# Last expert layer: rows stored by token and gathered by expert, slot owners from one-hot matmuls; router logits inside the norm, last group of residual norms by VectorE

## What is computed

```python
def _ln(x, g, b, eps=1e-05):
    mu = mean(x); v = mean((x - mu) ** 2)
    return (x - mu) * rsqrt(v + eps) * g + b

def _moe(x, wg, w1, b1, w2, b2):              # E = 8, FF = 1024
    S = L * N; cap = S // E                    # 2048 tokens, 256 rows per expert
    gates = softmax(xf @ wg); idx = argmax(gates)
    mask1 = one_hot(idx, E)
    loc = sum((cumsum(mask1, 0) - 1.0) * mask1, -1)    # place among the tokens of its expert
    keep = loc < cap
    slot = where(keep, idx * cap + loc, E * cap)
    disp = zeros((E * cap, D)).at[slot].set(xf, mode='drop')
    h = einsum('ecd,edf->ecf', disp, w1) + b1
    y = einsum('ecf,efd->ecd', h, w2) + b2
    return where(keep, gate_val * y[slot], 0.0)

y1 = _ln(x + _mha(x), ln1_g, ln1_b)
y2 = _ln(y1 + _moe(y1), ln2_g, ln2_b)          # and then x = x + y2
```

## Time and profile before

| | us |
|---|---|
| median of 3 runs | 2350.74 (2348.56 to 2352.39) |
| the profiled execution | 2351.17, its span 2349.3 |
| norm ahead of the last expert layer (`npa`) | 2124.5 to 2148.9 |
| its logits, routing and slots | 2148.9 to 2161.5 |
| scatters, loads, until the first expert's rows are turned | 2161.6 to 2188.7 |
| eight experts | 2188.7 to 2307.2 |
| returns, last norm, store | 2307.2 to 2349.3 |

### The profile page before, as it was taken

How to read it: one execution, slowest core, us unless ns; L and a number is a source line. 1 busy time by engine, 2 the same in 40 slices (tenths; PEclk the granted TensorE clock), 3 DMA queues, 4 the chain that set the end, 5 groups by cost and what they waited for, 6 DMA issues and landing times. The chain is left out here.

```text
span 2349.3 us, 38236 instructions
## 1 busy us (share of the span) xinstructions
PE 2057.0 (88%) x14629; PEld 1545.4 (66%) x14629; DVE 1252.7 (53%) x2505; ACT 1019.3 (43%) x2851; POOL 300.4 (13%) x392
## 2 busy tenths in 40 slices
PE   6789998899997689979999999978998998785795
PEld 4556666566665589766666667657886777663684
DVE  6457665788876144365554455655444555553113
ACT  3247774777775245333333333443222544333122
POOL 0101110222211524200000000031002000001212
PEclk8989999999999889989999999999999999997898
DMA  3000001121212633340000000010002000005352
GB/s 132 18 1 1 1 2 46 28 56 38 58 33 90 234 85 90 99 148 10 10 10 10 1 10 1 1 32 1 1 1 79 28 19 22 1 1 167 126 184 81
DMA packets 92564, 114.79 MB, mean 49 GB/s; under 512 B 20217, under 2 KB 75521, under 8 KB 91489
## 3 DMA queue, kind: packets, MB, share of 16 engines
q1 hardware_dynamic: 87440, 98.75, 13.8%
q0 software_dynamic: 4944, 13.59, 1.6%
HBM read 79.89 MB, written 25.08 MB: 45 GB/s over the span
## 5 line engine op out<-in xcount | busy, mean ns | idle before, releaser
L957 ACT ACTIVATE ca_prob<-bank,ca_nmax 128x512 f32<-128x512 f32 x256 | 174.2, 691 | 73.2 <-DVE ca_nmax L1024 73.2
L1024 DVE TENSOR_REDUCE ca_nmax<-bank 128x1 f32<-128x512 f32 x256 | 164.2, 683 | 40.9 <-PE bank L806 40.9
L957 ACT ACTIVATE na_prob<-bank,na_nmax 128x257 f32<-128x257 f32 x256 | 118.1, 474 | 148.4 <-DVE na_nmax L1024 148.4
L820 PE MATMUL bank<-cst,ca_prob 128*128 128x128 f32 x1024 | 140.6, 278 | 7.6 <-DVE ca_pT L1030 5.9
L820 PEld LDWEIGHTS bank<-cst,ca_prob 128*128 128x128 f32 x1024 | 111.0, 141 | 53.6 <-issue 44.9
L957 ACT ACTIVATE ra_prob<-bank,ra_nmax 128x256 f32<-128x256 f32 x256 | 118.4, 486 | 53.4 <-DVE ra_nmax L1024 53.4
L1024 DVE TENSOR_REDUCE na_nmax<-bank 128x1 f32<-128x257 f32 x256 | 90.9, 418 | 68.7 <-PE bank L806 68.7
L2267 PE MATMUL bank<-sf_h,sf_W 128*128 128x512 f32 x512 | 120.1, 395 | 0.0
L2267 PEld LDWEIGHTS bank<-sf_h,sf_W 128*128 128x128 f32 x512 | 95.9, 187 | 23.5
L2135 PE MATMUL bank<-na_Wkv,na_cxT 128*128 128x512 f32 x224 | 103.6, 605 | 0.0
L1024 DVE TENSOR_REDUCE ra_nmax<-bank 128x2 f32<-128x512 f32 x128 | 82.0, 683 | 39.6 <-PE bank L806 39.6
(11 more groups left out here) (475 smaller groups left out, 4611.9 us busy)
## 6 DMA issues: line engine op xcount, KB each, us to landing
xl_w<-in_L_ffn_w SPq DMA_DIRECT2D x16, 1024.0 KB, 7.6
rf_sent<-rf_w SPq DMA_DIRECT2D x13, 390.0 KB, 6.2
rf_xin<-rf_sent SPq DMA_DIRECT2D x39, 128.0 KB, 2.1
dp_cx<-in_ctx_tok SPq DMA_DIRECT2D x4, 1024.0 KB, 13.8
ca_v<-in_ctx_values SPq DMA_DIRECT2D x8, 512.0 KB, 4.8
rf_W<-in_L_ffn_w SPq DMA_DIRECT2D x8, 512.0 KB, 10.6
rf_rows<-rf_back SPq DMA_DIRECT2D x8, 512.0 KB, 5.6
na_Wkv<-in_L_xattn_Wkv SPq DMA_DIRECT2D x1, 4096.0 KB
```

Source lines behind the costliest of these rows:

```text
L820: mm = pe.transpose(TB[f % 2][:, j * P:(j + 1) * P], prob[:, n % 2, u, c0:c0 + P], ident)
L957: e = act.activation(prob[:, n % 2, u, hh * keys:(hh + 1) * keys], S[u][:, hh * keys:(hh + 1) * keys], ACT.Exp, bias=nmax[:, n % 2, u, hh: ...
L1024: v.tensor_reduce(nmax[:, n % 2, u], S[u][:, 0:W].rearrange("p (h k) -> p h k", h=per), AX.X, ALU.max, negate=True).then_inc(maxed, 1)
```

## The change

- Norm: the function gets `table`, an activation function whose table ScalarE loads after the last root by an operation on one column; `early` gets `shifted` as well. In the two residual norms GpSimd adds the shift to the last group of the residual at its start, and VectorE does the last group's gain and addition in one operation for each feature half, which replaces ScalarE's `affine` and GpSimd's addition of that group.
- Routed layer: the logits are computed at the end of the norm's block, for groups 0 to 2 first and then for group 3; Exp's table is loaded in the norm; `meta` is loaded after the first two row loads.
- Last expert layer: the same for logits and table. `sent` has 2048 rows of 257 (features, gate), stored by token number by four direct DMAs, and is not zeroed. The zero fills of `back` move from the norm's block to the beginning of the next, ahead of these stores. VectorE makes two one-hots for each token, `placed` (its place among 128) and `named` (its half of an expert's slots, times its channel and times its tile plus 1, in bf16); 16 matmuls add them into the owners of all 2048 slots. Unused slots fetch row 0 and keep a spare destination. GpSimd gathers two tiles for each expert by `fetch`, for expert e+2 ahead of the returns of expert e. The gates come with the rows (`gates`), `find_rows` uses the owner's number, and `meta` is gone.

```diff
@@ layer_norm_phase
 (SyncE)
+                        if gi == NG - 1:
+                            sp.wait_ge(added_last, KD)
+                        else:
+                            sp.wait_ge(added, KD * (gi + 1))
 (GpSimd)
-                    for gi in range(NG):
+                    last = part(resid, NG - 1)
+                    for k in range(KD):
+                        po.tensor_scalar(last[:, k], last[:, k], shift[:, k:k + 1], None, ALU.add).then_inc(shift_added, 1)
+                    for gi in range(NG - 1):
 (ScalarE)
+            if table is not None:
+                act.wait_ge(table_set, 1)
+                act.activation(g.hold[:], eps[:], table).then_inc(table_set, 1)
             if gain is not None:
-                affine(NG - 1)
-                act.wait_ge(shifted, KD * NG)
+                if resid is None:
+                    affine(NG - 1)
+                act.wait_ge(shifted, KD * (NG if resid is None else NG - 1))
 (VectorE)
+            if resid is not None:
+                v.wait_ge(shift_added, KD)
+                for k in range(KD):
+                    v.scalar_tensor_tensor(part(dst, NG - 1)[:, k], g.ln_cent[:, NG - 1, k], gain[:, k:k + 1],
+                                           part(resid, NG - 1)[:, k], ALU.mult, ALU.add).then_inc(added_last, 1)
@@ routed_ffn_layer
+        def early(pe, at, scaled, rooted, centred, shifted):
+            if at == NG:
+                pe.wait_ge(router, 16)
+                for some in (range(NG - 1), (NG - 1,)):
+                    pe.wait_ge(scaled, some[-1] + 1)
+                    for k in range(KD):
+                        for gi in some:
+                            mm = pe.matmul(g.bank[0][32 * gi:32 * gi + 32, :], Wr[:, k], g.XN[:, k, gi * GT:(gi + 1) * GT],
...
-                sp.dma_start(meta[:], sent[:, D:RW].rearrange("(t p) d -> p t d", p=P)).then_inc(meta_in, 16)
                 for i in range(NT):
...
+                    if i == 1:
+                        sp.dma_start(meta[:], sent[:, D:RW].rearrange("(t p) d -> p t d", p=P)).then_inc(meta_in, 16)
@@ expert_layer
+            def early(pe, at, scaled, rooted, centred, shifted):
+                if at == NG:
+                    pe.wait_ge(wl, 48)
+                    pe.wait_ge(centred, NG)
+                    for some in (range(NG - 1), (NG - 1,)):
+                        for k in range(KD):
+                            pe.wait_ge(shifted, KD * some[-1] + k + 1)
+                            for gi in some:
...
 (SyncE)
+                    for n in range(T // (4 * P)):
+                        sp.dma_start(back[1 + n * 4 * P:1 + (n + 1) * 4 * P, :].rearrange("(t p) d -> p t d", p=P),
+                                     zero[:, :, 0:D]).then_inc(emptied, 16)
+                    sp.wait_ge(gate_made, 1)
+                    for n in range(T // (4 * P)):
+                        sp.wait_ge(row_copied, 2 * n + 2)
+                        sp.dma_start(sent[n * 4 * P:(n + 1) * 4 * P, :].rearrange("(t p) d -> p t d", p=P),
+                                     rows[:, 4 * n:4 * n + 4]).then_inc(stored, 16)
 (GpSimd)
-                    for t in range(TT):
-                        po.indirect_dma_start(sent, bass.IndirectOffsetOnAxis(ap=slot[:, t:t + 1], axis=0), rows[:, t], None)\
-                          .then_inc(sent_all, 16)
+                    def gather(e):
+                        for t in range(2):
+                            n = 2 * e + t
+                            po.indirect_dma_start(xin[:, e % 2, t], None, sent,
+                                                  bass.IndirectOffsetOnAxis(ap=fetch[:, n:n + 1], axis=0)).then_inc(ldx[e % 2], 16)
+                    po.wait_ge(stored, 16 * (T // (4 * P)))
+                    po.wait_ge(st, 25)
+                    hold()
+                    gather(0)
+                    gather(1)
 (TensorE)
+                    pe.wait_ge(st, 20)
+                    for t in range(TT):
+                        if t % 4 == 0:
+                            pe.wait_ge(places_made, t // 4 + 1)
+                        mm = pe.matmul(g.bank[3][:, 0:32], placed[:, t], named[:, t], start=(t == 0), stop=(t == TT - 1))
+                    mm.then_inc(owners_found, 1)
 (ScalarE)
-                        if q == 5:
+                        if q == 4:
                             act.wait_ge(st, 3)
                             act.activation(pe8[:], dif[:], ACT.Exp).then_inc(eg, 1)
 (VectorE)
+                    v.tensor_scalar(upper[:], pos[:], float(P), None, ALU.is_ge).then_inc(st, 1)
+                    v.scalar_tensor_tensor(place[:], upper[:], -float(P), pos[:], ALU.mult, ALU.add).then_inc(st, 1)
+                    v.scalar_tensor_tensor(half[:], best[:], -float(HALVES), upper[:], ALU.mult, ALU.add).then_inc(st, 1)
...
+                    for q in range(4):
+                        ts = slice(4 * q, 4 * q + 4)
+                        v.tensor_tensor(placed[:, ts], g.c("iota")[:, 0:P].unsqueeze(1).to_broadcast([P, 4, P]),
+                                        place[:, ts].unsqueeze(2).to_broadcast([P, 4, P]), ALU.is_equal).then_inc(places_made, 1)
+                    v.wait_ge(owners_found, 1)
+                    v.tensor_copy(owner[:], g.bank[3][:, 0:32]).then_inc(st, 1)
+                    v.scalar_tensor_tensor(code[:], owner[:, 16:32], float(P), owner[:, 0:16], ALU.mult, ALU.add).then_inc(st, 1)
+                    v.tensor_scalar(fetchf[:], code[:], -float(P), 0.0, ALU.add, ALU.max).then_inc(st, 1)
+                    v.tensor_scalar(number[:], code[:], 1.0 - P, 0.0, ALU.add, ALU.max).then_inc(st, 1)
+                    v.tensor_copy(fetch[:], fetchf[:]).then_inc(st, 1)
```

More of the change, by code:

```diff
@@ L2619, in expert_layer @@
             rows = sb("rows", [P, TT, RW])
-            meta = sb("meta", [P, TT, 2])
-            empty, spare, row = (sb(n, [P, TT]) for n in ("empty", "spare", "row"))
+            empty, spare, row, upper, place, half, number, tile1, halves16, gates = (sb(n, [P, TT]) for n in (
+                "empty", "spare", "row", "upper", "place", "half", "number", "tile_plus_1", "halves_less_16", "gates"))
+            apart = sb("apart", [P, TT, 16])
+            placed = sb("placed", [P, TT, P], BF16)
+            named = sb("named", [P, TT, 32], BF16)
+            owner = sb("owner", [P, 32])
             dest = sb("dest", [P, TT], U32)
@@ L2630, in expert_layer @@
             loc = sb("loc", [P, TT, E])
-            mx, best, pos, keep, slotf, fetchf, lost, gate = (sb(n, [P, TT]) for n in (
-                "mx", "best", "pos", "keep", "slotf", "fetchf", "lost", "gate"))
-            slot = sb("slot", [P, TT], U32)
+            mx, best, pos, code, fetchf, gate = (sb(n, [P, TT]) for n in ("mx", "best", "pos", "code", "fetchf", "gate"))
+            fetch = sb("fetch", [P, TT], U32)
             w1 = sb("w1", [P, 2, KD, FF])
@@ L2727, in _ @@
[L2727 to L2734 removed]
+                    holds = 0
```

163 lines of the change are left out of this document (77 added, 86 removed).

## The result

The changed kernel takes 2327.15 us (median of four executions, 2322.93 to 2328.82), the kernel before 2349.65 on the same chip (2345.93 to 2352.39): a ratio of 0.9901, with an interval of 0.9883 to 0.9919. The forecast was 2324.5 with a range of 2320 to 2332. A repetition with six executions gave 2327.61 and 0.9893 (0.9868 to 0.9917).

The account below looks back on a forecast made before the run. One core runs the layers in sequence, with a 26 us stretch of GpSimd alone in the last expert layer. Terms of -20.8, -1.5, -2.0 and -1.9 sum to -26.2, giving 2324.5 us against the median, range 2320 to 2332.

Parts of the forecast that it names:

- The sum: Whole kernel: last expert layer -20.8, routed layer -1.5, two residual norms -2.0 and -1.9, together -26.2 us.
- Logits and block start: Last expert layer: logits inside the norm at 2.4 GHz, next block at 2149.0, -3.6 us, or -2.8 at 1.2 GHz.
- Table: Exp's table loaded in ScalarE's idle time in the norm: 1.7 us of wait saved in last layer, 1.3 in routed.
- Owners: Last expert layer: making the slot owners and fetch takes 5.6 us, with bounds of 4.6 and 7.
- The stores: Last expert layer: fills then stores end at 2161.9, wait over at 2162.7, first gather at 2163.5, bounds 2161.8 and 2166.
- The fills cost 1.7 here: Last expert layer: the zero fills of back ahead of the stores cost the first gather 1.7 us.
- The gathers: Last expert layer: two gathers priced like scatters, 1.27 apart and 2.91 to landing; TensorE turns rows at 2167.7, -21.0.
- rival 1: Last expert layer: stores and gathers slower than scatters suggest; layer gives -15 to -17, kernel 2329 to 2331; chance 0.20.
- Rivals 3 and 4: 3: slow gathers make GpSimd bound the experts, about 2358, chance 0.03; 4: stored comes late, 2344 to 2347, chance 0.03.
- Rival 2: Last expert and routed layers: TensorE runs both sets of logits at 1.2 GHz, kernel 2327; chance 0.12.
- Residual ends: Two residual norms: last group by VectorE instead of ScalarE and GpSimd, -2.0 in the first, -1.9 at the kernel's end.
- Routed layer: Scatters 2.5 us earlier, meta 1.0 later, TensorE's earlier turning gains nothing: together -1.5, from -3.0 to +0.5.

Follow-up runs that it names:

- six_banks: fills_in_norm with the routed layer's meta load ahead of its row loads and its key product in six TensorE banks instead of two: 2320.25 us, ratio 0.9877.
- before_again: The kernel before, without an edit, profiled a second time: 2345.09 us.
- no_tables: The changed kernel without the Exp table loads in the two norms, so Exp loads its table in the dispatch: 2328.19 us in one execution.
- fills_in_norm: The changed kernel with the four zero fills of back issued in the norm's block again: 2326.23 us, ratio 0.9892.
- gather1_late: fills_in_norm with the second expert's gathers held back until the first expert's have landed: 2320.55 us in one execution.
- no_early: The changed kernel with the last expert layer's logits after the norm, as before the change: 2326.94 us in one execution.
- old_resid: The changed kernel with the last group of both residual norms done by ScalarE and GpSimd again: 2329.16 us in one execution.
- wide: fills_in_norm with rows of sent of 1280 bytes instead of 1028: 2323.58 us in one execution.
- after_again: The changed kernel once more, without an edit: 2327.61 us over six executions, ratio 0.9893.

## Why the prediction was right, and where its sizes were off

**The sum.** 26.2 us were forecast, 22.5 came (2349.65 - 2327.15). By parts: last layer, S to the next norm, -17.3 for -20.8; null attention's norm -1.9 for -2.0, both from the gap to the next matmul; last norm -2.6 for -1.9; routed layer -2.8 in the first profile, but -0.9 to +4.0 in the ten other changed ones before six_banks (263.7, and 265.7 to 270.6 us, against 266.6 and 266.0), for -1.5. The first three make 21.8 of the 22.5. That the rest comes out so small is partly luck: the routed layer is longer than before in nine of these eleven profiles, and against before_again the last layer gained 19.6, not 17.3. One pair of profiles prices this layer only to some 2 us.

**Logits and block start: held.** The next block starts at S + 3.1, forecast 3.0, and the logits run at 2.4 GHz (PEclk 1.00 in 2134 to 2138, against 0.55 in the earlier trace rows). **Table: held.** Loaded in the gap before group 3; Exp follows without a wait. In no_tables it takes 1.28 us and Exp starts 0.02 behind it; the routed layer gains 1.4 by its removal. The drain of 1.38 us that the Trainium skill (ScalarE: Activation LUTs, What ACT_TABLE_LOAD costs) puts on top would have given 2.7: the trace disagrees. **Owners: held.** `fetch` is ready 11.8 us after the block's start, forecast 11.9; four `placed` took 2.49 rather than 2.7.

**The stores: right in kind, too small.** The step "the last byte at 2161.9, the wait over at 2162.7" priced fills and stores at 383 and 316 GB/s, 12.2 us from the first byte to the last. They took 14.4, from 2141.5 to 2155.9, in two stretches and a thin tail:

```profile
2141.50:2147.50 6.00, 3.35 (x32) 3.16 (x30) 4.62 (x18) 4.10 (x9) 0.00 (x0) 1.00 1.01 346
2147.50:2154.50 7.00, 1.14 (x16) 0.74 (x16) 4.95 (x17) 0.00 (x0) 0.00 (x0) 0.51 1.06 298
```

The stores' landing is seen 15.9 us after the block's start, not 13.7. The rate of the stores explains 0.5 of this (7.2 us alone in fills_in_norm, for 6.7); the rest appears only with fills and stores in the queue together, and why is open. "The fills cost 1.7 here" became 2.9 (fills_in_norm), and the first gather starts 4.4 us after `fetch`, not the 1 to 2 that the prediction named as a sign of being right. **The gathers: the same.** "2.91 from a start to its landing", taken from scatters, became 4.0 to the turn, also with nothing queued behind (gather1_late). First turn 21.6 us after the block's start for 18.7: 2.2 from the stores, 1.2 from the gathers (5.4 from the first start to the turn for 4.2), less 0.5 between landing and first gather. That is 2.9 of the 3.5 us by which the layer came short; the other 0.6 lies in the experts, the first of which took 9.06 us for its hidden matmuls against 8.57. It is rival 1 in its mechanism, at about half its size, so the forecast's range held it. Rivals 3 and 4 are out: gathers start 1.27 us apart, experts still take 14.25 us each. Rival 2 is out: the logits run at 2.4 GHz in both layers.

**What the logits and the table gave in the last layer.** The sum takes the first gather from the stores (2163.5), with `fetch` ready 1.8 us ahead of their landing (2160.9 and 2162.7). By those numbers the chain would have been late without the early logits and table, which are priced at about 3.6 and 1.7. Measured, `fetch` is ready 4.1 us ahead, so the stores hide nearly all of both: no_early costs 0.6 and no_tables nothing there.

**Residual ends: held.** 1.93 us each by old_resid. The end of the execution gained 2.6 between the profiles, 0.7 more than the pair of old_resid shows. The blocking that the Trainium skill (SBUF — State Buffer, Who interferes with whom) leads one to expect is not visible: L370 starts 0.04 us after the scaling beside a GpSimd addition with 0.05 to go, and its two operations take 1.42 us, of 0.69 forecast each. An overlap that short can't prove more.

**Routed layer: the start held, the end did not.** First scatter 3.2 us earlier (34.85 us after the norm's first matmul against 38.05; forecast 2.5), `meta` later by 0.9 (forecast 1.0). Part of the 3.2 is again the execution: in before_again the logits took 1.92 us rather than the 3.34 of the earlier trace rows, and the first scatter started at 36.41, so that 1.6 remains, of which the table alone makes 1.4 (no_tables). What failed is the step "TensorE's earlier turning gains nothing. Together -1.5", which took for granted that TensorE has finished the keys when the scatters end. In eleven of thirteen profiles it has not, in the kernel before either (before_again). Then the first turn hangs on the last late copy, up to 6 us behind the last scatter's start, and on one or two groups of keys, in part at 1.2 GHz. Whether the change made that worse (two groups left instead of one or none) two profiles of the kernel before can't tell. What holds the copies back stays open: the delays end with the scatters, which names a time, not a cause.

## What to carry to other kernels

When a scatter of rows is replaced by stores and a gather, price the stores from rows of the same length, in the queue that they will find, and the gather by a gather where there is one, and look which of the two inputs of the gather, rows or indices, lands last: work taken off the other one gains nothing. Zero fills belong ahead of the barrier, not in the queue of the stores that a gather waits for. And a filler that shares two banks between two engines beside a long run of indirect DMAs stalled until they were over in eleven of thirteen profiles; more banks are worth a try, though the one profile here doesn't prove them a cure. Look at several executions before giving a stage a price, since a single pair of profiles here held 4.3 us of clock and 6.5 us of this wait by accident.

## What the runs showed of the hardware that I had not expected

- Direct stores of 2048 rows in four DMAs: 7.2 us at 1028 bytes (fills_in_norm) and 7.5 at 1280 (wide), so that 25% more bytes cost 4% more time. In full flow 377 rows per us at 1024 bytes, 321 at 1028, 306 at 1280.
- An indirect gather of 128 rows of 1028 bytes: 0.96 us of GpSimd, 1.27 apart like a scatter, but 3.9 to 4.0 us from its start to TensorE's use of the rows; the scatters' landing took 2.9.
- Copies by ScalarE that started up to some 28 us after the matmuls that they wait for were recorded (27.3 in after_again: fifth group recorded by 795.78, copied at 823.04; 28.4 in no_early), while GpSimd's indirect DMAs ran; the last of them 5.6 to 5.9 us after the last scatter's start in eleven profiles.
- Loads of the Exp table: 1.28 us, with Exp 0.02 us behind; nothing more on the path (no_tables).
